# Thirty full expert tiles placed between the routing steps of the last batch

## What is computed

```python
h = layernorm(x) * (1 + ca) + sa
x = x + ga * attention(h)          # 16 heads of 8, causal, layer norm and Wo behind it
h = layernorm(x) * (1 + cb) + sb
bids = sigmoid(h @ conf_w.T + conf_b) * wealth        # 8 experts
top_bids, selected = top_k(bids, 2)
w = softmax(top_bids)
out = x + gb * sum over the 2 selected e of w_e * (silu(h @ gate_e.T) * (h @ up_e.T)) @ down_e.T
```

## Time and profile before

| what | us |
|---|---|
| median of 3 runs (lowest to highest) | 709.58 (706.45 to 715.05) |
| the profiled execution | 711.93 |
| its span | 710.0 |
| PE busy in the span | 604.5 |
| DVE busy | 474.6 |
| ACT busy | 392.7 |
| POOL busy | 315.3 |

### The profile page before, as it was taken

One profiled execution on the slowest core, in us unless ns is written; L12 is line 12 of the kernel. 1 busy time (PEld: TensorE's weight loads), 2 busy tenths in 40 slices (PEclk: granted clock), 3 DMA queues, 4 the chain that ended last, 5 costly groups with the idle time before them and its releaser, 6 DMA issues.

```text
span 710.0 us, 16028 instructions
## 1 busy us (share of the span) xinstructions
PE 604.5 (85%) x4887; PEld 412.4 (58%) x4888; DVE 474.6 (67%) x1576; ACT 392.7 (55%) x702; POOL 315.3 (44%) x445
## 2 busy tenths in 40 slices
PE   4789999999898998998989985208999999999940
PEld 1344444555454554554543534208999999999940
DVE  4898775888586696777875632734676666666635
ACT  1226765866675776667754583114655555556521
POOL 5114332456646647456565275561333333333325
PEclk9999998999999999999996796557999999999975
DMA  5716566453162342432521000121111111111137
GB/s 156 232 35 220 150 223 176 127 170 86 52 197 66 107 135 72 161 82 81 172 84 47 2 17 16 50 72 43 52 48 45 52 46 45 53 45 47 43 116 259
DMA packets 64887, 68.92 MB, mean 97 GB/s; under 512 B 8402, under 2 KB 55890, under 8 KB 64834
## 3 DMA queue, kind: packets, MB, share of 16 engines
q1 hardware_dynamic: 59938, 57.16, 27.4%
q0 software_dynamic: 4320, 8.99, 4.0%
q10 hardware_dynamic: 576, 2.10, 0.8%
HBM read 36.92 MB, written 31.03 MB: 96 GB/s over the span
## 4 chain that ended last, share of the span: by engine, by line
PE 74%; DVE 7%; DMA 5%; issue 5%; ACT 4%; POOL 2%; SPq 2%; another core or an unknown queue 0%; POOLq 0%; DVEq 0%; ACTq 0%
PE psN L698 18%; PE psO L504 11%; PE psN L473 10%; PE psT L487 10%; PE psO L709 9%; PE psN L475 3%; PE psM L512 2%; ACT probs L814 2%; DMA kst_all<-k_parts_dram 2%; DVE negm L1036 2%; PE psM L534 1%; PE psM L530 1%; PE psT L688 1%; PE psM L552 1%; DMA k_parts_dram<-kparts 1%
## 5 line engine op out<-in xcount | busy, mean ns | idle before, releaser
L1036 DVE TENSOR_REDUCE negm<-psN 128x1 f32<-128x512 f32 (+3 forms) x352 | 215.4, 636 | 86.4 <-PE psN L475 84.3
L814 ACT ACTIVATE probs<-psT 128x512 f32<-128x512 f32 x320 | 185.4, 598 | 92.2 <-PE psT L487 74.6
L473 PE MATMUL psN<-kst_all,qst_all 72*128 72x256 bf16 (+3 forms) x512 | 145.3, 321 | 9.3 <-DVE negm L1036 5.9
L698 PE MATMUL psN<-probs 128*128 128x128 f32 x1136 | 140.7, 278 | 0.0
L487 PE MATMUL psT<-qst_all,kst_all 74*128 74x384 bf16 (+3 forms) x512 | 126.1, 308 | 11.1 <-ACT probs L814 8.3
L698 PEld LDWEIGHTS psN<-probs 128*128 128x128 f32 x1136 | 134.7, 195 | 0.0
L1565 POOL DMA_INDIRECT expert_out<-kst_all,dest x71 | 68.8, 969 | 140.9 <-DVE kst_all L1367 137.2
L1458 POOL TENSOR_SCALAR_AFFINE_SELECT probs<-probs 128x512 f32<-128x512 f32 x128 | 80.0, 638 | 111.5 <-ACT probs L814 111.2
L473 PEld LDWEIGHTS psN<-kst_all,qst_all 72*128 72x128 bf16 x512 | 51.7, 102 | 92.4 <-issue 41.0
L475 PE MATMUL psN<-maskts,identb 128*128 128x128 bf16 x512 | 105.1, 230 | 0.0
L504 PE MATMUL psO<-probs,vaug 128*32 128x512 f32 (+3 forms) x1024 | 100.4, 466 | 1.0 <-POOL probs L1458 0.9
(11 more groups left out here) (214 smaller groups left out, 693.5 us busy)
## 6 DMA issues: line engine op xcount, KB each, us to landing
q_parts_dram<-qparts SPq DMA_DIRECT2D x24, 384.0 KB, 3.4
k_parts_dram<-kparts SPq DMA_DIRECT2D x24, 384.0 KB, 3.2
qst_all<-q_parts_dram SPq DMA_DIRECT2D x32, 288.0 KB
kst_all<-k_parts_dram SPq DMA_DIRECT2D x32, 288.0 KB
kst_all<-dispatched SPq DMA_DIRECT2D x71, 66.0 KB, 1.5
xall<-in_x SPq DMA_DIRECT2D x8, 256.0 KB, 4.2
gu_w<-in_gateT SPq DMA_DIRECT2D x4, 512.0 KB, 5.0
gu_w<-in_upT SPq DMA_DIRECT2D x4, 512.0 KB, 5.4
```

Source lines behind the costliest of these rows:

```text
L473: pe.matmul(psN[:, k % NBANKS, col:col + w], qst[g][0:KROWS, j, tb * P:(tb + 1) * P], kst[g][0:KROWS, j, 0:w], start=True, stop=False)
L698: mm = pe.matmul(bank[par][:, c * P:(c + 1) * P], ew[par][:, half, c * P:(c + 1) * P], xgT[par], start=True, stop=True)
L814: nc.scalar.activation(probs[:, g % 2, 512 * u:512 * (u + 1)], psT[:, u % TBANKS, :], ACT.Exp, scale=SOFTMAX_SCALE).then_inc(exp_done, 1)
L1036: nc.vector.tensor_reduce(dst, src, axis=AX.X, op=ALU.max, negate=True).then_inc(nat_done, 1)
```

## The change

After five batches are dispatched, their 5,120 pairs of token and expert fill at least 30 whole tiles, whatever the routing is. The changed kernel makes the table in two parts: the first 30 tiles (`N1`) from the counts of batches 0 to 4, during batch 7's attention, and the other 41 (`N2`) once all batches are counted. The stream of tiles starts directly behind the last attention step. The first 30 rounds are written out instead of looped, and the routing steps of batches 6 and 7 that stood between attention and experts stand in rounds 0 to 20 of them, on each engine at a round given by hand (`between(j)` on PE and ACT, `ahead(j)` and `behind(j)` on DVE, `ahead(j)` on POOL). The exponentials of the routing therefore stand between Silus on ACT. The pad blocks are written by SP between the loads of tiles 23 to 26. The normalising and modulating of batch 7 that DVE did goes to ACT (`h_norm`) and POOL (`h_scale`, `h_shift`). Batch 6's router moves from a bank of `psN` to one of `psT`, since `psN` holds gate and up results. The other 41 tiles are looped as before.

```diff
+HEAD = 5
+FULL_B = 5
+N1 = U * HEAD
+N2 = FTILES - N1
...
-            return psN[:, 0] if isinstance(b, int) and b == B - 2 else psM
+            return psT[:, 0] if isinstance(b, int) and b == B - 2 else psM
...
+            sp.wait_ge(dispatched, 16 * 2 * TB * FULL_B)
+            sp.wait_ge(t_full, UNITS * (STEPS - 2))
+            sp.wait_ge(tiles_ready, 1)
+            for j in range(N1):
+                tile_in(*divmod(j, U))
+                if N1 - 7 <= j < N1 - 3:
+                    pads_out_of(2 * (j - N1 + 7))
+                    pads_out_of(2 * (j - N1 + 7) + 1)
             sp.wait_ge(pads_out, 16 * (1 + NX))
+            sp.wait_ge(tiles_ready, 2)
             sp.wait_ge(dispatched, 16 * 2 * NT)
...
+            def between(j):
+
+                if j == 0:
+                    turn_values(L, 3)
+                if j == 3:
+                    turn_attn(L)
+                    turn_h(L - 1)
+                if j == 4:
+                    project_o(L)
+                if j == 5:
+                    experts(L - 1)
+                if j == 9:
+                    turn_h(L)
+                if j == 10:
+                    rank(L - 1)
+                    experts(L)
+                if j == 15:
+                    rank(L)
+                if j == 17:
+                    count_all()
...
+            pe.wait_ge(exp_done, UNITS * STEPS)
             turn_in(0, 0)
+            for j in range(N1):
+                turn_in(*divmod(j + 1, U))
+                gate_up(*divmod(j, U))
+                between(j)
+                if j > 0:
+                    down(*divmod(j - 1, U))
+            pe.wait_ge(tiles_ready, 2)
+            with pe.Fori(HEAD, TURNS - 1) as i:
...
+                if j == 2:
+                    o_norm(L)
+                if j == 3:
+                    keep_attn(L)
+                    keep_h(L - 1)
+                if j == 6:
+                    keep_z(L - 1)
+                if j == 7:
+                    h_norm(L)
+                if j == 9:
+                    keep_h(L)
+                if j == 10:
+                    exp_bids(L - 1)
+                    keep_z(L)
+                if j == 14:
+                    exp_bids(L)
...
+                    if (b, g, k) == (B - 1, 2, 9):
+                        table(slice(0, N1), nfull, None)
+                        V.nop().then_inc(tiles_ready, 1)
...
+                if j == 7:
+                    for i in range(5):
+                        route(L - 1, i)
...
+                if j == 18:
+                    dve.wait_ge(count_full, 2)
+                    link(V.tensor_copy(padslots[:], psM[:, 0:NX]))
+                    V.nop().then_inc(dispatch_ready, 1)
+                    link(V.tensor_tensor(counts[:], psM[:, 0:NX], base[:], ALU.subtract))
+                    tiles_of(ntile)
...
+                if j == 20:
+                    table(slice(N1, FTILES), nfull, nhead[:, 0:1])
+                    V.nop().then_inc(tiles_ready, 1)
...
+                if j == 5:
+                    h_inv(L)
+                if j == 6:
+                    h_scale(L)
+                    h_shift(L)
+                if j == 8:
+                    count(L - 1)
+                if j == 10:
+                    scatter(L - 1, (0,))
+                if j == 11:
+                    scatter(L - 1, (1,))
+                if j == 12:
+                    scatter(L - 1, (2,))
+                if j == 13:
+                    count(L)
+                    scatter(L - 1, (3,))
+                if 16 <= j < 16 + TB:
+                    scatter(L, (j - 16,))
```

More of the change, by code:

```diff
@@ L590, in rank, with count_head, count_all @@
                           start=False, stop=True).then_inc(slot_full, 1)
+            def count_head():
+                take((head_counted, 1))
+                pe.wait_ge(taken_chain, 5 * FULL_B + 1)
+                pe.matmul(psM[:, 0:NX], ones[:], taken[:, TB], start=True, stop=True).then_inc(count_full, 1)
+            def count_all():
+                take()
+                pe.wait_ge(taken_chain, 5 * B + 1)
+                pe.matmul(psM[:, 0:NX], ones[:], taken[:, TB], start=True, stop=True).then_inc(count_full, 1)
             def step(b, g):
@@ L668, in _ @@
                 values(L, 3, c)
-            turn_values(L, 3)
-            turn_attn(L)
-            turn_h(L - 1)
-            project_o(L)
-            experts(L - 1)
-            turn_h(L)
-            rank(L - 1)
-            experts(L)
-            rank(L)
-            take()
-            pe.matmul(psM[:, 0:NX], ones[:], taken[:, TB], start=True, stop=True).then_inc(count_full, 1)
+            def between(j):
[17 more added lines that the diff above has]
+                    count_all()
             def turn_in(i, u):
@@ L715, in at, with turn @@
                 return i + u // U, u % U
-            def turn(i, first=False, last=False):
+            def turn(i, last=False):
                 for u in range(LAST if last else U):
@@ L721, in turn @@
                     gate_up(i, u)
-                    if not (first and u < 1):
-                        down(*at(i, u - 1))
+                    down(*at(i, u - 1))
             pe.wait_ge(tiles_ready, 1)
+            pe.wait_ge(exp_done, UNITS * STEPS)
             turn_in(0, 0)
-            turn(0, first=True)
-            with pe.Fori(1, TURNS - 1) as i:
+            for j in range(N1):
[6 more added lines that the diff above has]
+            with pe.Fori(HEAD, TURNS - 1) as i:
                 turn(i)
@@ L940, in _ @@
             act.wait_ge(tiles_ready, 1)
+            act.wait_ge(pv_done, TB * (STEPS - 1))
             keep_weights(0, 0)
-            turn(0)
-            with act.Fori(1, TURNS - 1) as i:
+            for j in range(N1):
+                if j == N1 - 1:
+                    act.wait_ge(tiles_ready, 2)
+                keep_weights(*divmod(j + 1, U))
+                silu(*divmod(j, U))
+                between(j)
+            with act.Fori(HEAD, TURNS - 1) as i:
                 turn(i)
@@ L1308, in _ @@
-            link(V.tensor_tensor(over_thr, over(counts[:], [P, NX, NT]), thr[:].unsqueeze(1).broadcast_to([P, NX, NT]),
-                                 ALU.is_gt))
-            link(V.tensor_reduce(ntile[:], over_thr, axis=AX.X, op=ALU.add))
-            link(V.memset(cums[0][:, 0:4], 0.0))
-            link(V.memset(cums[1][:, 0:4], 0.0))
-            link(V.tensor_copy(cums[0][:, 4:], ntile[:]))
-            a, c = cums
-            for sh in (1, 2, 4):
-                link(V.tensor_tensor(c[:, 4:], a[:, 4:], a[:, 4 - sh:4 + NX - sh], ALU.add))
-                a, c = c, a
@@ L1330, in keep_tile, with behind @@
+            def behind(j):
+                if j == 0:
+                    normalise(L, 3)
+                    dve.wait_ge(og_done, 4 * B)
+                    stats(on, stO, so_chain, range(TB))
+                    mean_var(stO, mvO, so_chain, L, onn_ready)
             def keep_tile(i, u):
@@ L1376, in turn @@
                     multiply(i, u)
-                    if not (first and u < 1):
-                        weigh(*at(i, u - 1))
+                    weigh(*at(i, u - 1))
                     weights(i, u)
             keep_tile(0, 0)
-            turn(0, first=True)
-            with dve.Fori(1, TURNS - 1) as i:
+            for j in range(N1):
+                keep_tile(*divmod(j + 1, U))
+                ahead(j)
+                multiply(*divmod(j, U))
+                behind(j)
+                if j > 0:
+                    weigh(*divmod(j - 1, U))
+                weights(*divmod(j, U))
+            with dve.Fori(HEAD, TURNS - 1) as i:
                 turn(i)
@@ L1566, in send @@
                                       ysb[u], None).then_inc(y_out[u], 16)
-            with pool.Fori(0, TURNS - 1) as i:
+            for j in range(N1):
+                ahead(j)
+                send(*divmod(j, U))
+            with pool.Fori(HEAD, TURNS - 1) as i:
                 for u in range(U):
```

186 lines of the change are left out of this document (114 added, 72 removed).

## The result

The changed kernel took 682.72 us, the kernel before 708.65 (medians of 6 runs each, 678.53 to 687.37 and 706.45 to 715.05): ratio 0.9622, 95% interval 0.9559 to 0.9685. Forecast was 673 in a range of 664 to 688. The gain is 26 us where the forecast said 36.6 (709.58 - 673; its sum before rounding has 36.9).

The account below looks back on a forecast made before the run. PE bounds the tile stream, and a routing chain leaves 53 us between attention and experts. 711.93 - 48.6 + 6.5 + 0.7 + 1.5 + 1.5 + 1.5 = 675.0 us, stated as 673, range 664 to 688.

Parts of the forecast that it names:

- three signs of being wrong: PE waits over 10 us in the head, first group starts after 437 us, or attention ends later than 431.
- the first rival: Head rounds with links: lateness never recovers, each of 21 loses about 0.8 us, 17 instead of 4.5, so 685 us; chance 0.13.
- Start of the stream, -48.6: Between attention and experts: first gate/up group starts at 433.7 us instead of 482.28, saving 48.6 us.
- PE's chain work, +6.5: In the head: PE's transposes, projection, scorings, ranks and count, formerly under the chain, now add 6.5 us; bounds 5 and 14.
- Attention side, +0.7: During attention: new DVE work, an extra count matmul and pad memsets cost 0.7 us together; bounds 0 and 6.
- ACT, +1.5: In the head: table loads, exponentials and normalising on ACT make PE wait 1.5 us; bounds 0 and 8.
- POOL, +1.5: Head, round 15: batch 7's count, behind sends and scatters, ends 1.5 us after PE asks; bounds 0 and 5.
- DVE, +1.5: Head rounds 18 to 20: counting, sums and the 41-tile table make DVE late, costing 1.5 us; bounds 0 and 5.
- rival of the dear switch: ACT in the head: each table switch takes its 1.28 us twice, about 7 us in all, 680 us; chance 0.11.
- figures near 681 and 667: Whole time: clock low for long, near 681, chance 0.07; clock and lateness both better, near 667, chance 0.04.
- ring through POOL: Head: held-back sends make DVE, PE and links wait in a ring; 730 us at 3 us a round; chance 0.05.
- C: Experiments' candidate, not a forecast term: pad rows' DMA traffic near 503 us causes the stalls between 501 and 520, 9 to 10 us.

Follow-up runs that it names:

- c1: e8's head, with extra POOL row scatters behind it in the steady stream, single and three back to back; 646.21 us, 0.946 of the kernel before.
- e3: Changed kernel with the exponentials of batches 6 and 7 made linear, so the head has no table loads; 651.01 us, ratio 0.950.
- e6: e8 with the sigmoid and two-way softmax of batches 6 and 7 computed by Tanh, needing no table load in the stream; 685.41 us, ratio 0.962.
- e4: Changed kernel with the nine pad-row DMAs moved behind the load of tile 29; 657.33 us, ratio 0.962.
- m1: Changed kernel with 24 extra POOL row scatters in rounds 30 to 65, four back to back every sixth round; 653.57 us, ratio 0.956.
- m3: m2 with the extra scatters' rows of 512 bytes instead of 528; 656.55 us, ratio 0.960.
- e1: Changed kernel with all 16 row scatters of batches 6 and 7 together in round 28; 676.34 us, ratio 0.987.
- e2: Changed kernel with the 16 row scatters of batches 6 and 7 one per round instead of two; 647.37 us, ratio 0.948.
- m2: Changed kernel with 24 extra POOL row scatters in rounds 30 to 65, one each in four of six rounds; 658.63 us, ratio 0.964.
- a0: Changed kernel again, unaltered; 687.46 us, ratio 0.964 to the kernel before on that chip.
- b0: Kernel before again, unaltered, for its profile on another chip; 705.1 us.
- e8: e2 with the table over 41 tiles made in four pieces in rounds 20 to 23 instead of all in round 20; 682.15 us, ratio 0.957.

## Why the prediction was right, and where its sum was off

The time is in the range and the mechanism is the one forecast: the 53 us filled with tiles, PE's chain work added, and waits at the places named. But the gain is 26 us and not 36.6, and one of the prediction's three signs of being wrong came: PE waits 10.5 us in the head of the first profile, where the three waits of the sum make 4.5 us and over 10 were to mean wrong. (The first group starts at 435.3, before 437, and attention ends at 430.6, before 431.) On chips without late signals the same head has 5.3 us of waits. So it was the width of the range, whose upper part was meant for the first rival, that took in a loss which no term had. By step:

- **Start of the stream, -48.6.** Measured -47.0. In c1, without late signals, the last values end at 403.16 + 1.72 = 404.88 and the first group starts at 408.07, 3.2 us later; the sum had 4.3, with 0.6 us for the tile's expert number, whose load in c1 (0.48 + 0.17 us in ACT's queue, from 405.04 on) runs beside the last copy (404.96 + 0.60) and the table load behind it (405.57 + 1.28). In the first profile it was 4.7, in the main since the copy of the last values came 1.5 us late: this row, in ACT's order of time, answers to the 430.16 of the earlier trace rows.

```profile
432.17 0.60 ACT L868 ACTIVATE oT<-psO 128x512 f32<-128x512 f32 x1 [3.05 <-remote]
432.78 1.28 ACT L997 ACT_TABLE_LOAD   x1
434.08 2.00 ACT L978 ACTIVATE probs<-gu_w 128x1024 f32 x2
```

- **PE's chain work, +6.5.** In c1 the head is 91.6 - 83.7 = 7.9 us over the tiles, with 0.4 + 0.8 of waits in it (the other 0.5 of the 0.9 lies ahead of the first group): 6.7. Right.
- **Attention side, +0.7.** The last values end at 430.6 instead of 429.4, on a chip where such a difference cannot be told from lateness. Not contradicted, and not shown.
- **ACT, +1.5.** 0.8 by the stretch from tile 8 to 10 in e3 and e6. The six loads are there, 1.28 us each, and mostly hidden, as the step said.
- **POOL, +1.5.** This step failed in size: 3.8 us on chips without late signals, 4.0 to 5.6 with the round behind it. The count was late by 2.2 us, close to the 1.5 of the step; the low clock behind the wait was in no term.
- **DVE, +1.5.** The wait is 1.9 us, and costs 2.1 (e4, m1, m3) or, where the clock falls, 3.7 (e1, e2, e3, m2).
- **What no term had.** Stalls, that is waits and what the lower clock adds, of about 16 us in the first profile (23.9 less 6.7, less about 1 for the first gate/up group, 3.24 us at 435.28 against 2.02 in c1) against 4.5 of the sum. On chips without late signals they are 8 to 11 (heads of 97.9 to 101.0). The rest, some 6 to 9 us, is put down to the late signals and the clock behind them, since it is there only on chips that have them. No run takes them away on one chip.

The first rival (rounds late throughout, 685) lies nearest to the measured time, but not by its mechanism: the rounds recover, PE is full from 440 to 480, and in c1 the links cost 1.2 us of waits in the whole head. The loss is in a few places. The rival of the dear switch is refuted. The row that follows a load between full neighbours was what the earlier trace rows lacked:

```profile
458.60 1.28 ACT L891 ACT_TABLE_LOAD   x1
459.89 0.20 ACT L891 ACTIVATE en<-psT 128x32 f32<-128x32 f32 x1
...
461.05 1.28 ACT L986 ACT_TABLE_LOAD   x1
462.35 0.60 ACT L986 ACTIVATE probs<-psN 128x512 f32<-128x512 f32 x1
```

The next activation starts 1.29 and 1.30 us after the load does, and each load starts 0.01 us after the activation ahead of it has ended (457.99 + 0.60, 459.99 + 1.05). So a switch takes 0.02 to 0.03 us beside its row of 1.28, not another 1.28. The figures near 681 and 667 with the clock in them are the author's estimates. The clock was low in pieces behind waits (0.50 to 0.70 for some 3 us in e2, 0.50 for 3 us in m1), not in one long stretch. At the start it is low in the kernel before, but not always in the changed one: on the chips without late signals c1 and e2 start at the full clock (first group 2.02 us instead of 3.62), e1, e3 and m1 do not (2.94, 2.97 and 3.45 us). The ring through POOL did not form: in m1 POOL works without a gap from 451.7 to 469.3 us and then waits for DVE again, 2.0 us. (The case against the ring counts 14 scatters in 21 rounds. The code has 16, which makes its sum 54 of 65 us.)

## What to carry to other kernels

When work is filled between the links of a chain, look in each in-order queue for the one item that a link waits for, and put nothing long ahead of it: one scatter a round instead of two and a table in four pieces took the 14 to 17 us that a head had over its tiles down to 8, on chips without late signals. Give a wait of PE of about 2 us a range from once to twice its length: here the same 1.9 us cost 2.1 in three runs and 3.7 in four, by whether the matmuls behind it ran at the lower clock. And before a wait is put down to the engine that the profile names, look whether that engine had long been done.

## What the runs showed of the hardware that was not expected

Chips differ by 3.6 to 4.7% on the same kernel: medians of 682.5 to 684.3 us on three, 708.65 on that of the first profiles and 714.53 on that of a0, b0, e8 and e6. The slower ones show late signals: waits of 0.9 to 5.7 us of ACT or DVE, nearly all on work of PE that had ended before, mostly within 4 us behind POOL's row scatters and never in the steady stream with one send per tile. Of the two marks of the slower chips, the waits and the scatters ahead of them, only the first is shown to depend on the chip. Whether scatters set it off there stays open: the extra scatters never ran on such a chip. The wait at 506.67 lies in a stretch with the pads' 528 KB DMA under way as well, so C is open for it too: the pads were moved only on a chip without late signals.

The clock falls behind a short wait in one run and not in the next. Behind the same 1.9 us wait of PE it went to 0.50 in e1, e2, e3 and m2 and stayed at 1.00 in e4, m1 and m3, and the rounds of tiles 21 and 22 took 9.3 us or 7.7.
